# Projection and attention as one block, eight loads for each adapter pack, and the split of the base weights shared between VectorE and GpSimd

## The chip, the cores and the metric

One core of one Trainium2 chip. The metric is the device time of one launch in microseconds. The kernel before takes 848.53 us (median of three runs, 847.76 to 848.71).

## The reference

Input x has 8 sequences of 128 tokens with 512 features. Four stages follow one another, each adds its result to x:

```
x1 = x  + x  @ W0[id]^T                                  # one 512x512 base weight per sequence
x2 = x1 + attention(x1)                                  # 32 query heads, 8 key/value heads, D = 128, RoPE, causal
     q,k,v,o = x @ w + (x @ a[id]) @ b[id]               # rank-16 adapters a, b picked per sequence
x3 = x2 + (x2 @ B2[id]) @ A2[id]
out = x3 + x3 @ W3^T + b3 + 2 (x3 @ A3[id]) @ B3[id]
```

## The kernel before

Every float32 product is made of three products of rounded operands: each operand is split into a high part (a copy on ScalarE into the type float32r) and a low part (raw minus high, on VectorE or GpSimd), and TensorE adds hi*hi, hi*lo and lo*hi. The text calls these copies and low parts.

**First block (lines 210 to 768), 38 steps `s`.** At step s TensorE does the base product of sequence s (`product`, 12 matmuls), the adapter products `x1 @ a` of sequence s-1 (`adapters`), the transposition of x1 of sequence s (`turn_x1`, L693) and unit n = s-2 of the projections (`values`, `project`). Units 0 to 15 are values (two blocks of 512 columns, 8 sequences each, first matmul L730), units 16 to 31 keys, units 32 to 35 the queries of the first group (first matmul L78, `project`). The base weight of sequence s+1 is split at step s: ScalarE copies it in two halves (L391), VectorE makes the low parts (L491), and only then adds the product of sequence s to x (`add`, L497), for which `turn_x1` waits. For steps 1 to 7 the weight of the next sequence therefore stands in the chain of the step.

The raw base weights have three buffers (`w0_raw`), the adapters A three (`RAW = 3`). All loads of this block are issued by SyncE in one written order: `load_w0(b)` (xt and the base weight, 1 MB), `load_x`, `load_a`, and between them the projection blocks, `load_block_w` (1 MB, L166) and `load_block_b` (L176), which fills a **pack**. A pack holds the rows of the adapter B of all 8 sequences, each sequence's 16 rows four times (two for the high part and two for the low part), so that one more matmul per unit adds the adapter. `load_block_b` reads the id of each sequence and issues four loads of 16 partitions for it, 32 in all:

```
for quad in range(4):
    at = 32 * quad + R * (b % 2)
    dma.dma_start(raw_b[at:at + R, b // 2, :], src[bass.DynSlice(pick, 1), :, cols]...)
```

The first pack stands in SyncE's order ahead of `load_x(1)`, the second ahead of `load_w0(7)`, the third and fourth behind all base weights; the fourth stands ahead of the stores of rotated keys (`k_rot`, L348). The pack of the first queries comes from a tensor gathered by GpSimd (`bq_sel`) in four loads of 32 partitions (L180). `PIECES` says at which step each quarter of a block or pack is copied (ScalarE, L425 and L430) and gets its low part (VectorE, L514 and L519). Keys and first queries are rotated by VectorE (L609, L611) and added by GpSimd (L668). Values go to HBM by stores of ScalarE from three buffers.

**Second block (from line 770), 8 groups `g` of 8 slots.** A slot is one sequence of one group of four heads: scores (L1091), mask and maximum (VectorE), exponential (ScalarE), division (GpSimd, L966), transposition (L1100), values (L1108 to L1110), output projection with `wo` (L1122 to L1124) and its adapter `ao_pack` (L1131), and one query head of the next half (`queries`, `project`). Query heads are rotated by VectorE (L991, L993) and added by GpSimd (L959). Within the slots the weights of the next group are split: `wq` by ScalarE and GpSimd (L951), the query pack by ScalarE and VectorE (`bq_lo_part`, L999, low rows 64 to 127 only), `wo` by ScalarE, and its four low quarters by VectorE (0 in slot 1 and 1 in slot 2, L1004) and GpSimd (2 and 3 in slot 1, L976), followed by the low part of `ao_pack` (L979). `outputs` of slot 0 is issued in slot 2 and waits for the quarters one by one. Groups 1 to 6 are a hardware loop. Each block ends with a barrier of all engines. A third block makes the last two stages.

Of the kernel before, what the change touches and what calls it, by code (L numbers as in the profile page):

```python
# [7 lines left out]
P = 128  # L8
F32 = mybir.dt.float32
# [7 lines left out]
NEG = -1.0e30  # L17
# [13 lines left out]
def program(nc, x, xt, lora_ids, pos, attn_ids, slot_ids, mask, w0, wq, wk, wv, wo, a3, bq, bk, bv, ao, bo,  # L31
            l2a, l2b, w3, b3, l3a, l3b, ident_c, causal_c, rope_c, gather_c, twin_c, out):
# [20 lines left out]
    bq_sel = nc.dram_tensor("bq_sel", (B, R, KVH * GW), F32, kind="Internal").ap()  # L53
# [10 lines left out]
    with whole:  # L64
# [30 lines left out]
        twin = sb(whole, "twin", [P, 3])  # L95
        l2b_sel = sb(whole, "l2b_sel", [P, KC, B, R])
# [28 lines left out]
        axn = [sb(early, f"axn{i}", [P, 3, 4, 2, R], F32R) for i in range(2)]  # L125
# [9 lines left out]
        raw_b_in = sem(attn, "raw_b_in")  # L135
# [28 lines left out]

        def load_block_w(dma, j):
# [17 lines left out]
        RAW_B_IN = (512, 1024, 1536, 2048, 2048 + 64)  # L183

# [3 lines left out]
        def load_bq(dma, g, h):  # L188
            for quad in range(4):
                dma.dma_start(raw_b[32 * quad:32 * quad + 32, 2 * h:2 * h + 2, :],  # L190
                              bq_sel.rearrange("(c two) r n -> (two r) c n", two=2)[:, 2 * h:2 * h + 2, bass.DynSlice(g * GW, GW)]
                              ).then_inc(bq_in[h], 16)
# [12 lines left out]
        with ExitStack() as c:  # L205
            for i in (1, 2):
# [5 lines left out]
            RAW = 3  # L212
# [7 lines left out]
                     for flat, at in ((l2a_flat, 0), (l2a_flat, 3 * KC * R), (l2b_flat, 0))]  # L220
# [9 lines left out]
            ps_y = [ps(c, f"ps_y{i}", [P, HID]) for i in range(2)]  # L230
            ps_x1 = ps(c, "ps_x1", [P, KC, T])
            ps_ax = ps(c, "ps_ax", [P, 4, T])
            ps_a = ps_ax[:, 0, 0:3 * R].rearrange("p (n r) -> p n r", r=R)
            ps_at = ps_ax[:, 1:4, :]
            ps_p = [ps(c, f"ps_p{i}", [P, GW]) for i in range(4)]

            lora_ids_in = sem(c, "lora_ids_in")
            ids_in = sem(c, "ids_in")
            w0_first_in = [sem(c, f"w0_first_in{k}") for k in range(KC)]
            consts_in = sem(c, "consts_in")  # L240
            x_in = [sem(c, f"x_in{b}") for b in range(B)]
            xt_in = [sem(c, f"xt_in{i}") for i in range(RAW)]
            w0_in = [sem(c, f"w0_in{i}") for i in range(RAW)]
            a_in = [sem(c, f"a_in{b}") for b in range(B)]
            ident_ready = sem(c, "ident_ready")
            xt_hi_done = sem(c, "xt_hi_done")
            xt_lo_done = sem(c, "xt_lo_done")
            wt_hi_done = sem(c, "wt_hi_done")
            wt_lo_done = sem(c, "wt_lo_done")
            y_ready = sem(c, "y_ready")  # L250
            x1_done = sem(c, "x1_done")
            x1t_ready = sem(c, "x1t_ready")
            x1t_hi_done = sem(c, "x1t_hi_done")
            x1t_lo_done = sem(c, "x1t_lo_done")
            zeroed = sem(c, "zeroed")
            a_hi_done = sem(c, "a_hi_done")
# [1287 lines left out]
```

## Time and profile before

| | before |
|---|---|
| median of runs | 848.53 us |
| profiled execution, its own time | 849.5 us |
| its span | 847.8 us |
| TensorE matmul busy | 755.8 us (89%) |
| VectorE busy | 536.1 us (63%) |
| ScalarE busy | 324.8 us (38%) |
| GpSimd busy | 294.1 us (35%) |
| mean rate of transfers | 104 GB/s |
| mean granted TensorE clock | 0.956 of full speed |

The span is the time from the first to the last instruction; the execution's own time has 1.7 us more. Busy times overlap. A row of the timeline gives start, length, engine, line, operation, output and inputs, the count of merged instructions, and in brackets how long the engine sat idle before it and what ended that.

### The profile page before, as it was taken

The page shows a single profiled execution, that of the slowest core. Times are in us where ns is not written, and L with a number is a line of the kernel's source. Part 1 is how long each engine was busy: PE and PEld are TensorE (multiplying, and loading weights), DVE is VectorE, ACT ScalarE, POOL GpSimd, SP SyncE. Part 2 cuts the span into 40 slices and gives each one's busy share as a digit, 9 for nine tenths or more (in the row PEclk, how much of TensorE's full clock was granted, in tenths as well). Part 3 has the DMA queues.
Part 4 walks back from the last instruction along what each step waited for, and adds up shares of the span by engine and source line. Part 5 has one row for each costly group of instructions (what it writes and reads, how often), then busy time and mean ns, then how long its engine had stood idle before and what let it go on. Part 6 is the DMA issues. An engine that isn't in the chain of part 4 may idle for free. (4 is left out here: it accounts for less than half of the span.)

```text
span 847.8 us, 13367 instructions
## 1 busy us (share of the span) xinstructions
PE 755.8 (89%) x4100; PEld 623.1 (73%) x4100; DVE 536.1 (63%) x1370; ACT 324.8 (38%) x902; POOL 294.1 (35%) x265
## 2 busy tenths in 40 slices
PE   3292989879779999999999999999999999998798
PEld 2282877657567887887887888788788788876586
DVE  3251558756866667657566667666765756654883
ACT  4261525112053435335344435343534533433550
POOL 1020325253545236235326335423623532420220
PEclk8587899989889999999999999999999999999899
DMA  6573678546604122303303302312130310620502
GB/s 218 215 267 94 193 239 269 157 157 191 215 9 137 39 63 66 109 16 108 111 0 108 127 0 62 136 38 62 65 108 21 103 37 0 151 26 2 128 14 87
DMA packets 63083, 87.88 MB, mean 104 GB/s; under 512 B 20086, under 2 KB 37654, under 8 KB 59334
## 3 DMA queue, kind: packets, MB, share of 16 engines
q1 hardware_dynamic: 44338, 73.54, 28.0%
q10 hardware_dynamic: 17044, 8.46, 3.3%
q0 software_dynamic: 1664, 5.44, 2.1%
q8 instruction: 17, 0.28, 0.1%
q14 instruction: 20, 0.16, 0.1%
HBM read 72.45 MB, written 19.68 MB: 109 GB/s over the span
## 5 line engine op out<-in xcount | busy, mean ns | idle before, releaser
L966 POOL TENSOR_TENSOR prob<-prob,rinv 128x512 f32<-128x512 f32 x64 | 66.6, 1040 | 255.3 <-DVE rinv L1054 255.3
L907 ACT ACTIVATE ot_hi<-ps_o 128x512 fp32r<-128x512 f32 x64 | 38.1, 595 | 222.1 <-PE ps_o L1110 222.1
L1122 PE MATMUL ps_out<-wo_hi,ot_hi 128*128 128x512 f32 x256 | 102.8, 402 | 10.4 <-DVE wo_lo L1004 5.7
L959 POOL TENSOR_TENSOR qt<-qc,qs 128x512 f32<-128x512 f32 x60 | 77.9, 1298 | 70.0 <-DVE qs L993 70.0
L917 ACT ACTIVATE prob<-sm,nmax 128x128 f32<-128x128 f32 x256 | 99.8, 392 | 6.2 <-DVE nmax L1035 4.5
L1123 PE MATMUL ps_out<-wo_lo,ot_hi 128*128 128x512 f32 x256 | 101.3, 396 | 0.0
L1124 PE MATMUL ps_out<-wo_hi,ot_lo 128*128 128x512 f32 x256 | 100.8, 394 | 0.0
L78 PE MATMUL ps_q<-x1t_hi,wgt_hi 128*128 128x512 f32 x240 | 100.4, 418 | 0.0
L80 PE MATMUL ps_q<-x1t_hi,wgt_lo 128*128 128x512 f32 x240 | 95.4, 398 | 0.0
L79 PE MATMUL ps_q<-x1t_lo,wgt_hi 128*128 128x512 f32 x240 | 95.2, 397 | 0.0
L1032 DVE MEMSET gate<- 128x1 f32 x64 | 3.8, 59 | 136.9 <-PE ps_s L1091 136.9
L993 DVE TENSOR_TENSOR qs<-ps_q,trig 64x512 f32<-64x512 f32 x120 | 82.6, 689 | 3.7
L1091 PEld LDWEIGHTS ps_s<-kt,qt 128*128 128x128 f32 x512 | 66.6, 193 | 17.5 <-issue 10.3
L1091 PE MATMUL ps_s<-kt,qt 128*128 128x128 f32 x512 | 69.9, 280 | 7.5 <-PEq L286 6.8
L1122 PEld LDWEIGHTS ps_out<-wo_hi,ot_hi 128*128 128x128 f32 x256 | 48.2, 188 | 24.8 <-DVE wo_lo L1004 9.2
L1035 DVE CUSTOM_DVE_ANT_0 sm<-ps_s,maskbias 128x128 f32<-128x128 f32 x256 | 59.1, 286 | 0.9 <-issue 0.2
L1124 PEld LDWEIGHTS ps_out<-wo_hi,ot_lo 128*128 128x128 f32 x256 | 48.0, 187 | 11.6
L901 ACT ACTIVATE pt_hi<-ps_t 128x512 fp32r<-128x512 f32 x64 | 38.2, 596 | 44.1 <-PE ps_t L1100 44.1
L1123 PEld LDWEIGHTS ps_out<-wo_lo,ot_hi 128*128 128x128 f32 x256 | 48.3, 188 | 8.1
L80 PEld LDWEIGHTS ps_q<-x1t_hi,wgt_lo 128*128 128x128 f32 x240 | 45.4, 189 | 10.7
L78 PEld LDWEIGHTS ps_q<-x1t_hi,wgt_hi 128*128 128x128 f32 x240 | 45.8, 191 | 8.0
L79 PEld LDWEIGHTS ps_q<-x1t_lo,wgt_hi 128*128 128x128 f32 x240 | 45.7, 190 | 8.1
(193 smaller groups left out, 1720.2 us busy)
## 6 DMA issues: line engine op xcount, KB each, us to landing
raw_w<-in_wq SPq DMA_DIRECT2D x8, 1024.0 KB, 5.3
wo_raw<-in_wo SPq DMA_DIRECT2D x8, 1024.0 KB, 4.9
raw_b<-bq_sel SPq DMA_DIRECT2D x56, 128.0 KB, 5.2
qt<-in_w SPq DMA_DIRECT2D x5, 1024.0 KB, 6.8
v_hi_d<-v_hi ACTq DMA_DIRECT2D x16, 256.0 KB, 4.6
v_lo_d<-v_lo ACTq DMA_DIRECT2D x16, 256.0 KB, 5.1
kt<-k_rot SPq DMA_DIRECT2D x16, 256.0 KB, 2.6
v_hi<-v_hi_d SPq DMA_DIRECT2D x16, 256.0 KB, 3.2
```

What stands on the lines that cost most here:

```text
L78: pe.matmul(bank[:, :], w_hi[:, k, cols], x1t_hi[:, k, tok], start=(k == 0), stop=False)
L79: pe.matmul(bank[:, :], w_hi[:, k, cols], x1t_lo[:, k, tok], start=False, stop=False)
L80: pe.matmul(bank[:, :], w_lo[:, k, cols], x1t_hi[:, k, tok], start=False, stop=False)
L917: e = act.activation(prob[i][:, h, :], sm[:, h, :], ACT.Exp, bias=nmax[i][:, h:h + 1], scale=-1.0, accum_out=rsum[i][:, h:h + 1])
L959: pool.tensor_tensor(qt[:, half, h, :], qc[:, :], qs[:, :], ALU.add).then_inc(q_done, 1)
L966: pool.tensor_tensor(prob[i][:, :, :], prob[i][:, :, :], rinv[i][:, :].unsqueeze(2).broadcast_to([P, G, T]), ALU.mult).then_inc(prob_done, 1)
L993: dve.tensor_tensor(qs[to:to + 64, :], ps_q[i][at:at + 64, :], sin_t[to:to + 64, tok], ALU.mult).then_inc(q_mult, 1)
L1035: m = dve.tensor_tensor_reduce(out=sm[:, h, :], in0=ps_s[i][:, h, :], in1=maskbias[:, b, :], scale=-1.0, scalar=3.0e38, op0=ALU.add, op1=A ...
L1091: mm = pe.matmul(ps_s[b % 2][:, h, :], qt[:, half, h, at:at + T], kt[:, b * T:(b + 1) * T], start=True, stop=True)
L1122: pe.matmul(ps_out[:, :], ot_hi[:, q], wo_hi[:, h, :], start=(h == 0), stop=False)
L1123: pe.matmul(ps_out[:, :], ot_hi[:, q], wo_lo[:, h, :], start=False, stop=False)
L1124: pe.matmul(ps_out[:, :], ot_lo[:, q], wo_hi[:, h, :], start=False, stop=(h == G - 1))
```

## The change

It moves these things:

- The first and second block become one: the functions `project_sync`, `project_scalar` and so on are called at the head of each engine's part of the attention block, and the barrier between them is gone. The PSUM banks are shared between the parts (`ps_y` and `ps_s`, `ps_p` and `ps_out`, `ps_o`, `ps_q`), and explicit waits take the barrier's place.
- A pack has 8 loads of 64 partitions that read 16 rows four times, in each of the three places that fill `raw_b`. The order of rows in a pack changes with it, the low rows are no longer one half, and VectorE makes them with one instruction over 128 partitions. Each pair of sequences has a semaphore of its own.
- The first pack is spread: pair 0 behind `load_a(1)`, pair 1 behind `load_a(2)`, pairs 2 and 3 behind `load_a(3)`.
- GpSimd makes the last quarter of the low part of each base weight from the second on; VectorE makes three quarters.
- The adapters A have four raw buffers (`AR = 4`).
- In the attention loop `bq_lo_part` stands behind the rotation, VectorE makes one low quarter of `wo` a group and GpSimd three, and ScalarE copies all four quarters of `wo` ahead of `ot`.

```
-        def load_block_b(dma, j):
+        def load_block_b(dma, j, pairs):
...
-            for b in range(B):
+            for b in range(2 * pairs[0], 2 * pairs[-1] + 2):
                 pick = dma.value_load(id_rows[0:1, 1, b:b + 1], min_val=0, max_val=src.shape[0] - 1)
-                for quad in range(4):
-                    at = 32 * quad + R * (b % 2)
-                    dma.dma_start(raw_b[at:at + R, b // 2, :], src[bass.DynSlice(pick, 1), :, cols].rearrange("a r n -> (a r) n")).then_inc(raw_b_in, 16)
+                four_times(dma, b, src[bass.DynSlice(pick, 1), :, cols], raw_b_in[b // 2])
+
+        def four_times(dma, b, rows, done):
+
+            dma.dma_start(raw_b[4 * R * (b % 2):4 * R * (b % 2 + 1), b // 2, :], rows.broadcast_to([4, R, GW])).then_inc(done, 16)
...
         def load_bq(dma, g, h):
-            for quad in range(4):
-                dma.dma_start(raw_b[32 * quad:32 * quad + 32, 2 * h:2 * h + 2, :],
...
+            for b in range(HALF * h, HALF * (h + 1)):
+                four_times(dma, b, bq_sel[bass.DynSlice(g, 1), b], bq_in[h])
...
+                def split_w0_end(b):
+                    k = KC - 1
+                    pool.wait_ge(wt_hi_done, wt_parts(b, k))
+                    pool.tensor_tensor(wgt_lo[1 + b % 2][:, k, :], w0_raw[b % RAW][:, k, :], wgt_hi[1 + b % 2][:, k, :].bitcast(F32),
+                                       ALU.subtract).then_inc(wt_lo_end, 1)
...
+                        if b and k == KC - 1:
+                            pe.wait_ge(wt_lo_end, b)
...
                     def bq_lo_part(n, p):
                         dve.wait_ge(bq_hi_done, n)
-                        lo = slice(P // 2, P)
-                        dve.tensor_tensor(bq_pack[lo, p, :], bq_raw[lo, p, :], bq_pack[lo, p, :].bitcast(F32),
-                                           ALU.subtract).then_inc(bq_lo_done, 1)
+                        dve.scalar_tensor_tensor(bq_pack[:, p, :], bq_pack[:, p, :].bitcast(F32), lows[:, 0:1], bq_raw[:, p, :],
+                                                 ALU.mult, ALU.add).then_inc(bq_lo_done, 1)
...
                     def scores(t, g, b):
                         half = b // HALF
+                        if isinstance(t, int) and t == 0:
+                            pe.wait_ge(k_done, VU + G)
```

**SyncE, first loads.** Before, from the load of the first value block on (`raw_w<-in_wv`); the third base weight is the load `trig<-in_w`, and it comes after seven more groups like the one for `raw_b` shown here:

```order
L166 DMA raw_w<-in_wv 128x2048
L173 TENSOR_LOAD id_rows
L173 ISA x2
L176 ISA
L176 DMA raw_b<-in_bv 16x512 x4
L173 TENSOR_LOAD id_rows
L173 ISA x2
L176 ISA
L176 DMA raw_b<-in_bv 16x512 x4
```

Now, from the first load of the pack to the same base weight, behind `load_x(1)` and `load_a(1)`:

```order
L187 DMA raw_b<-in_bv 64x1x512
L182 TENSOR_LOAD id_rows
L182 ISA x2
L187 ISA
L187 DMA raw_b<-in_bv 64x1x512
L302 TENSOR_LOAD id_rows
L302 ISA x2
L313 DMA l3a_sel<-in_xt 128x512
L314 ISA
L314 DMA trig<-in_w 128x2048
```

Two loads of a pack stand ahead of the third base weight instead of 32, and `load_x(1)` stands ahead of both.

**VectorE, slot 1 of a group in the attention loop.** Before:

```order
L1008 TENSOR_TENSOR pt_lo<-ps_t,pt_hi 128x512
L999 TENSOR_TENSOR pack<-raw_b,pack 64x512
L1054 RECIPROCAL rinv<-rsum 128x4
L991 TENSOR_TENSOR qc<-ps_q,trig 128x512
L993 TENSOR_TENSOR qs<-ps_q,trig 64x512 x2
L1004 TENSOR_TENSOR wo_lo<-wo_raw,wo_hi 128x512
```

Now:

```order
L1022 TENSOR_TENSOR pt_lo<-ps_x_t,pt_hi 128x512
L1064 RECIPROCAL rinv<-rsum 128x4
L1006 TENSOR_TENSOR qc<-ps_p_q,trig 128x512
L1008 TENSOR_TENSOR qs<-ps_p_q,trig 64x512 x2
L1013 SCALAR_TENSOR_TENSOR pack<-pack,lows,raw_b 128x512
L1018 TENSOR_TENSOR wo_lo<-wo_raw,wo_hi 128x512
```

The low part of the pack has moved from ahead of the reciprocal to behind the rotation, and covers 128 partitions.

## Rows read from the trace of the kernel before

**Rows 1.** Waits of TensorE, 0 to 240 us: waited for, total, times, longest

```profile
PE ps_ax L716 <- DVE axn L507: 19.2, 3, 16.4
```

**Rows 2.** Timeline of TensorE: transpositions that open steps 1, 2, 3 and 7

```profile
41.41 1.12 PE L693 MATMUL ps_x<-ident,res 128*128 128x128 f32 x4 [16.16 <-DVE res L497]
...
51.76 0.66 PE L693 MATMUL ps_x<-ident,res 128*128 128x128 f32 x4
...
59.59 0.66 PE L693 MATMUL ps_x<-ident,res 128*128 128x128 f32 x4
...
110.12 0.66 PE L693 MATMUL ps_x<-ident,res 128*128 128x128 f32 x4
```

**Rows 3.** Timeline of SyncE's queue: issue start, length of all issues

```profile
10.37 19.34 SPq L176 DMA_DIRECT2D raw_b<-in_bv  x32
...
32.43 0.34 SPq L310 DMA_DIRECT2D trig<-in_w  x1
...
63.14 19.05 SPq L176 DMA_DIRECT2D raw_b<-in_bv  x32
...
155.88 19.70 SPq L176 DMA_DIRECT2D raw_b<-in_bk  x32
...
202.27 1.83 SPq L180 DMA_DIRECT2D raw_b<-bq_sel  x4
```

**Rows 4.** Timelines of ScalarE, VectorE and GpSimd: base weights, table loads

```profile
14.40 2.00 ACT L391 ACTIVATE wgt_hi<-qt 128x1024 fp32r<-128x1024 f32 x2 [1.90 <-DMA qt<-in_w]
...
37.31 1.06 ACT L391 ACTIVATE wgt_hi<-trig 128x1024 fp32r<-128x1024 f32 x1 [2.27 <-DMA trig<-in_w]
...
38.40 2.36 DVE L491 TENSOR_TENSOR wgt_lo<-trig,wgt_hi 128x1024 fp32r<-128x1024 f32 x2 [5.87 <-ACT wgt_hi L391]
...
62.36 1.06 ACT L391 ACTIVATE wgt_hi<-trig 128x1024 fp32r<-128x1024 f32 x1
...
99.67 0.55 POOL L650 DMA_DIRECT2D rope_cols<-in_rope_c  x1
...
110.88 0.75 DVE L527 TENSOR_SCALAR trig<-qt,rope_cols 128x1024 f32<-128x1024 int32 x1
```

**Rows 5.** One stretch: length, busy PE, PEld, DVE, ACT, POOL, clock, share, GB/s

```profile
60.00:65.00 5.00, 5.00 (x26) 4.18 (x25) 3.05 (x5) 4.26 (x8) 1.85 (x2) 1.00 1.02 342
```

**Rows 6.** Transfer issues by the page: count, size of each, us to landing

```profile
raw_b<-bq_sel SPq DMA_DIRECT2D x56, 128.0 KB, 5.2
...
raw_b<-bq_sel SPq DMA_DIRECT2D x4, 256.0 KB, 5.0
```

**Rows 7.** Timeline of TensorE: first matmul of key and query units

```profile
154.72 0.47 PE L78 MATMUL ps_p<-x1t_hi,wgt_hi 128*128 128x512 f32 x1 [3.37 <-DVE pack L519]
...
168.48 0.40 PE L78 MATMUL ps_p<-x1t_hi,wgt_hi 128*128 128x512 f32 x1
...
171.53 0.39 PE L78 MATMUL ps_p<-x1t_hi,wgt_hi 128*128 128x512 f32 x1
...
226.87 0.40 PE L78 MATMUL ps_p<-x1t_hi,wgt_hi 128*128 128x512 f32 x1
```

**Rows 8.** Timelines of TensorE and GpSimd at the block boundary

```profile
236.91 0.55 PE L1091 MATMUL ps_s<-kt,qt 128*128 128x128 f32 x1 [6.84 <-PEq L286]
...
232.32 1.26 POOL L668 TENSOR_TENSOR qt<-qt 128x512 f32<-128x512 f32 x1 [1.76 <-DVE qt L611]
```

**Rows 9.** Attention: TensorE's wait on `wo_lo` (whole run), and slots 1 and 2 of group 2

```profile
PE ps_out L1122 <- DVE wo_lo L1004: 5.7, 8, 0.9
...
383.18 0.69 DVE L999 TENSOR_TENSOR pack<-raw_b,pack 64x512 fp32r<-64x512 f32 x1
...
387.60 1.65 DVE L1004 TENSOR_TENSOR wo_lo<-wo_raw,wo_hi 128x512 fp32r<-128x512 f32 x1 [1.51 <-ACT wo_hi L891]
...
388.66 3.02 POOL L976 TENSOR_TENSOR wo_lo<-wo_raw,wo_hi 128x512 fp32r<-128x512 f32 x2
...
393.52 0.50 PE L1122 MATMUL ps_out<-wo_hi,ot_hi 128*128 128x512 f32 x1 [0.87 <-DVE wo_lo L1004]
```

More of the change, by code:

```diff
@@ L95, in program @@
         twin = sb(whole, "twin", [P, 3])
+        lows = sb(whole, "lows", [P, 1])
         l2b_sel = sb(whole, "l2b_sel", [P, KC, B, R])
@@ L124, in program @@
         a_lo = [sb(early, f"a_lo{i}", [P, KC, 3, R], F32R) for i in range(2)]
-        axn = [sb(early, f"axn{i}", [P, 3, 4, 2, R], F32R) for i in range(2)]
+        axn = [sb(early, f"axn{i}", [P, 3, 2, 4, R], F32R) for i in range(2)]
         early.close()
@@ L134, in program @@
         raw_w_in = sem(attn, "raw_w_in")
-        raw_b_in = sem(attn, "raw_b_in")
+        raw_b_in = [sem(attn, f"raw_b_in{p}") for p in range(PAIRS)]
         wq_in = sem(attn, "wq_in")
@@ L240, in program @@
[L240 to L249, printed above, removed]
@@ L274, in program @@
-            k_out = [sem(c, f"k_out{i}") for i in range(2)]
-            tables_in = sem(c, "tables_in")
-            tab = sem(c, "tab")
-            sines = sem(c, "sines")
+            ps_a = ps_ax[:, 0:3 * R].rearrange("p (n r) -> p n r", r=R)
+            ps_at = ps_ax[:, T:4 * T].rearrange("p (n t) -> p n t", t=T)
+            lora_ids_in = sem(attn, "lora_ids_in")
+            ids_in = sem(attn, "ids_in")
+            w0_first_in = [sem(attn, f"w0_first_in{k}") for k in range(KC)]
+            consts_in = sem(attn, "consts_in")
@@ new lines, in program @@
+            x_in = [sem(attn, f"x_in{b}") for b in range(B)]
+            xt_in = [sem(attn, f"xt_in{i}") for i in range(RAW)]
+            w0_in = [sem(attn, f"w0_in{i}") for i in range(RAW)]
+            a_in = [sem(attn, f"a_in{b}") for b in range(B)]
+            ident_ready = sem(attn, "ident_ready")
+            xt_hi_done = sem(attn, "xt_hi_done")
+            xt_lo_done = sem(attn, "xt_lo_done")
+            wt_hi_done = sem(attn, "wt_hi_done")
+            wt_lo_done = sem(attn, "wt_lo_done")
@@ L279, in parts @@
+            v_out = [sem(attn, f"v_out{i}") for i in range(VR)]
+            k_mult = sem(attn, "k_mult")
+            k_done = sem(attn, "k_done")
+            k_out = [sem(attn, f"k_out{i}") for i in range(2)]
+            tables_in = sem(attn, "tables_in")
+            tab = sem(attn, "tab")
+            sines = sem(attn, "sines")
             def parts(b):
@@ L920, in slots @@
                             if b < HALF and not last:
+                                if first and b == 0:
+                                    act.wait_ge(p_ready, KU + G)
                                 act.wait_ge(q_ready, B * g + b + 1)
@@ L931, in slots @@
                                     act.wait_ge(out_ready, B * g)
-                                wo_hi_part(g, 0)
-                                wo_hi_part(g, 2)
+                                for h in range(G):
+                                    wo_hi_part(g, h)
                             if not first or b >= 1:
@@ L1044, in slots @@
                                 pt(t - 1)
-                            if b == 2:
-                                wo_lo_part(g, 1)
-                            if not last and b % 2:
-                                bq_lo_part(PAIRS * g + b // 2 + 1, b // 2)
                             dve.wait_ge(exp_done, t + 1)
@@ L1056, in slots @@
                                 rotate(t, (b // HALF + 1) % 2, i)
+                            if not last and b % 2:
+                                bq_lo_part(PAIRS * g + b // 2 + 1, b // 2)
                             if b == 1:
```

989 lines of the change are left out of this document (491 added, 498 removed).

## The prediction

> **What bounds the kernel now.** Read the waits of TensorE over the first 240 us first. It is held 19.2 us by the adapter block `axn`, 16.4 of them at once [rows 1]; the row with 16.16 us in its brackets [rows 2] is a second hold, by `res`. TensorE is the busiest engine (89%), so idle time of it outside the attention loop is the time to be won. Those waits name VectorE, but VectorE is only the last link. The queue of SyncE shows the first one: the 32 loads of a pack take 19.34, 19.05 and 19.70 us to issue [rows 3], and whatever stands behind them in the program waits for that. The load of the third base weight goes out at 32.43 for this reason alone [rows 3], is copied from 37.31 on, and the transposition of step 1 starts 4.1 us later at 41.41 [rows 2, 4]. The pack issued from 63.14 does the same to the last base weight: TensorE's wait of 16.4 us on `axn` [rows 1]. The pack issued from 155.88 holds back the stores of rotated keys. In the attention loop TensorE works without pause except for one wait on `wo_lo` a group, 5.7 us in 8 places [rows 9].
>
> **Undisturbed pace, the yardstick for the sum.** In the first stage a step, from one transposition to the next, takes 51.76 to 59.59, 7.83 us, when nothing is late; right after the long hold it takes 41.41 to 51.76, 10.35 us, at TensorE's low level, so a hold costs 2.5 us more than itself [rows 2]. A key or query unit takes 3.05 us (168.48 to 171.53) [rows 7].
>
> **Issue of a pack.** A pack now has 8 loads. 32 loads in 19.34 us with 8 id reads; the four of one sequence therefore take 2.42 us. A load that carries 128 KB is issued in 1.83/4 = 0.46 us [rows 3], so the id read is about 2.42 - 4 x 0.41 = 0.8 us and a pack costs 8 x (0.8 + 0.4) = 9.6 us instead of 19.3. Only one pair of the first pack stands ahead of the third base weight, which then goes out near 14.7 instead of 32.43.
>
> **How long a pack occupies the transfer engines.** The trace has no load of 64 partitions that reads 16 rows four times, so bound it. At the rate of a full queue, 342 GB/s in 60 to 65 us [rows 5], its 1.05 MB take 3.1 us. Two batches of four 128 KB loads, each landing 5.2 us after its issue [rows 6], give about 10.4 us at most. Nearest is the pack of four 256 KB loads at 202.27: the same tile, whole, with 32 partitions each; issued over 1.8 us and landing 5.0 after [rows 3, 6], near 7 us. I take 7.4 and keep 3.1 and 10.4 as ends. The Trainium skill, "DMA: Bandwidth & Descriptors", Rules for kernel authors, speaks against this form of load: an outermost dimension of c copies confines a transfer to at most c of the 16 engines, here 4. By it, an estimate from that page and the 342 GB/s, a pack takes 12 us and the sum comes out some 9 us later than mine; no row shows such a transfer.
>
> **Step 1.** The second base weight landed at 14.40 [rows 4]. Behind it now stand x and the adapter A of sequence 0, the first value block, x and A of sequence 1, xt and the third base weight: 3.08 MB by their shapes, 9.0 us at 342 GB/s, and a quarter of a pack, 1.85 us. It lands at 25.2. From landing to the transposition the trace has 4.1 us; VectorE's second low part is half as long (1.2 to 0.6 us [rows 4], the last quarter goes to GpSimd beside it), so 3.5 us: 28.7 instead of 41.41. **Gain 12.7.** In undisturbed steps that same 0.6 us is worth nothing: TensorE is busy throughout, and it covers VectorE.
>
> **Steps 2 to 7.** Each step needs its weight about 3 us after the transposition that opens it (59.59, copy at 62.36 [rows 2, 4]; I allow 0.2 us more). A sequence's transfers are 1.67 MB, 4.9 us; a value block 3.1 us; a step's two stores 1.5 us. Landings: third 25.2, fourth 25.2 + 4.9 + 1.85 = 32.0, fifth (half a pack and a store) 42.1, sixth 48.5, seventh (value block) 58.0, eighth (a whole pack) 71.8. Transpositions at 28.7, 39.0 (10.35 later, for TensorE has just been held), 46.9, 54.7 and 62.5, so the weights are needed at 31.7, 42.0, 49.9, 57.7 and 65.5. All but the eighth come within 0.3 us. The eighth is 6.3 us late; with 2.5 us of low clock the transposition of step 7 starts at 39.0 + 5 x 7.83 + 6.3 + 2.5 = 87.0 instead of 110.12 [rows 2]. That is 23.1 less, so **10.4 more**. GpSimd now splits a last quarter before it issues the table loads, some 3.5 us later by my estimate (it waits for ScalarE's second copy of the step, then works 1.3 us). It issued the last at 99.67 and VectorE first used them at 110.88 [rows 4]; 11.2 less 3.5 still covers a landing of 5 to 6 us, so I cost it at nothing, and a longer landing would show in full.
>
> **Values to the first key unit.** Gathers, value stores, tables and the waits around 148 to 154 us stand in the same order with the same bytes. I take 0.
>
> **Keys and first queries.** From 154.72 to 226.87 are 18 units in 72.15 us [rows 7]; undisturbed 18 x 3.05 = 54.9. Loss 17.3, of which 1.5 us is the low clock after the wait that ends at 154.72 and stays. The rest came from the pack at 155.88 and from the query pack at 202.27. The first now frees SyncE near 165.5 instead of 175.6. GpSimd wants the first key store's landing about then, and TensorE runs four banks ahead. The query pack now has a semaphore for each pair, so two pairs are enough to start. I give back 0.8 us for stores that queue behind a pack: **15.0**. VectorE's low part over all 128 partitions is priced as over 64: the time goes by the 512 columns.
>
> **The boundary.** TensorE restarts at 236.91 after 6.84 us [rows 8]. Without a block boundary the scores still need the last rotated query, which GpSimd makes at 232.32 + 1.26 = 233.6 [rows 8]; the last unit ended near 230.1 (236.91 - 6.84): **3.3**. Late next is that rotation itself.
>
> **Attention.** VectorE no longer makes the second quarter of `wo_lo` late in slot 2; GpSimd makes three in slot 1. It did two from 388.66 in 3.02 us [rows 9]; a third and the adapter part at 1.3 each end at 394.3. TensorE had been ready for the second quarter at 392.65 and reaches the adapter 2.1 us later, 394.7: just covered. So the waits of 0.87 in six groups and their restart, 1.1 a group with the weight load, go: 6.6. Against that, `bq_lo` moves behind the rotation, where it meets GpSimd's addition. One such meeting is in the trace, 1.65 us for a VectorE part that takes 0.69 alone [rows 9]. The Trainium skill, "SBUF — State Buffer", Who interferes with whom, has it that the one that starts second is fully blocked when both read two tiles of SBUF; by that GpSimd would be 0.7 us later at each meeting. In the trace GpSimd's surplus at such a meeting is 0.5 us at most (two quarters in 3.02 us, 1.3 each alone). It can reach TensorE at the two slots of a group whose scores need the rotation just made, and part of it is made up by a reciprocal 0.7 us earlier: of 0 to 0.5 I take 0.2 x 13 = 2.6. **Net 4.0.**
>
> **Sum.** 23.1 + 15.0 + 3.3 + 4.0 = 45.4 us. 847.8 - 45.4 = 802.4 span; the profiled execution took 849.5, 1.7 more than its span and 1.0 more than the median of 848.53, so 803.1: **803**.
>
> **Rivals.**
> *Packs at full rate.* If four copies spread as any load, a pack takes 3.1 us and the eighth weight lands 8.6 us earlier: no hold in steps 2 to 7, and no low clock; step 1 gains 1.1 more. Then 803 - 6.3 - 2.5 - 1.1 - 1 (keys) = 792. For it: 2 KB rows throughout, as before. Against: the pack at 202.27 took twice that.
> *Packs at 10.4 us or more.* Two packs lie before the eighth weight: 2 x 3 = 6 us, and about 2 in keys: 811. It decides if a 128 KB load holds its engines over 1.3 us.
> *Issue does not shrink.* If the issue time went by rows, 64 against 16, a pack would still take 19 us. Left are the new place of the first pair (about 10), the boundary and attention: 803 + 24 = 827. Against it: loads of 128 partitions are issued in the same 0.3 to 0.5 us.
> *Slower: the lock in the attention loop.* 28 slots get the moved part behind the rotation. If each meeting cost both its surpluses, 1.65 - 0.69 = 0.96 on VectorE and 3.02 - 2 x 1.28 = 0.46 on GpSimd [rows 9], and all of it reached TensorE, and GpSimd's third quarter cost 1.3 in each of 8 groups on top, the loop would lose 28 x 1.42 + 10.4 = 50 us instead of gaining 4.0; the kernel would take 848.5 - 41.4 + 50 = 857. It decides from 41 us on, 0.7 us a slot. Against: at most 2 of 8 slots wait for a rotation at all.
>
> **Chances.** The forecast 0.50, full rate 0.25, slow packs 0.17, issue unchanged 0.05, lock 0.03. A measurement of this kernel tells about 0.2%, 1.7 us, from no change; the first four are all faster by more: faster 0.97, same 0, slower 0.03. The range runs from 5 us under the full-rate case to 5 us over the slow packs, 787 to 816, and leaves out the last two cases and tails of the others.
>
> **What would show it.** The pack's issue near 9.6 us; the third base weight issued near 15 and the transposition of step 1 near 29; a single hold before step 6 of about 6 us and none elsewhere in the first stage; no wait over 1 us among the keys after the first two; scores 3.5 us after the last query unit; no wait on `wo_lo`. A hold of 12 us means slow packs, none at all means full rate. Wrong would be a longer stretch between the last base product and the first key, which I left untouched, or slots over 8.4 us.

## The result, and the profile after

| | before | change |
|---|---|---|
| median of runs (lowest to highest) | 848.62 us (847.76 to 851.34) | 822.80 us (820.86 to 829.19) |
| ratio to before, 95% interval | | 0.9704, 0.9646 to 0.9761 |
| profiled execution, its span | 847.8 us | 819.2 us |
| TensorE matmul busy | 755.8 us (89%) | 752.1 us (92%) |

The kernel became faster, by 26 us where 45 were forecast; 822.8 lies above the range of 787 to 816. The two spans differ by 28.6 us. Cut at the same five places in both traces they show where the gain is and where it is missing (the last column is the first experiment below):

| stretch | before | forecast | change | rows outermost |
|---|---|---|---|---|
| start to the transposition of step 1 | 41.41 | 28.7 | 29.38 | 29.14 |
| on to the transposition of step 7 | 68.71 | 58.3 | 59.36 | 52.50 |
| on to the second key unit | 44.60 | 44.6 | 46.82 | 43.22 |
| on to the last query unit (18 units) | 72.15 | 57.2 | 74.34 | 63.88 |
| on to the first scores | 10.04 | 6.7 | 6.76 | 6.76 |
| on to the end of the span | 610.9 | 606.9 | 602.5 | 606.9 |

So the first stage and the boundary came nearly as forecast, the loop gave more, and the keys, from which I expected 15.0 us, lost 2.2. The table is of one profiled execution each; the change's repeat (experiment 5) has 30.43, 61.03, 44.51 and 72.54 us in the first four stretches. The rows behind that begin with SyncE's queue in the change (start, length of the issues, engine and line, output and input, count), to be held against [rows 3]:

```profile
12.20 2.69 SPq L187 DMA_DIRECT2D raw_b<-in_bv  x2
16.52 0.35 SPq L314 DMA_DIRECT2D trig<-in_w  x1
...
51.44 14.41 SPq L187 DMA_DIRECT2D raw_b<-in_bv  x8
67.56 0.35 SPq L314 DMA_DIRECT2D qt<-in_w  x1
...
136.68 13.75 SPq L187 DMA_DIRECT2D raw_b<-in_bk  x8
...
179.44 4.62 SPq L187 DMA_DIRECT2D raw_b<-bq_sel  x8
```

The third base weight (`trig`) goes out at 16.52 instead of 32.43, as meant. But a pack of eight loads takes about 14 us to issue, not 9.6. The transpositions that open steps 1 and 7, in TensorE's timeline, against 41.41 and 110.12 in [rows 2]:

```profile
29.38 1.12 PE L708 MATMUL ps_x_t<-ident,res 128*128 128x128 f32 x4 [2.83 <-DVE res L502]
...
88.74 0.66 PE L708 MATMUL ps_x_t<-ident,res 128*128 128x128 f32 x4
```

TensorE's waits from 0 to 240 us, grouped (waited for, total, times, longest), against [rows 1]: the 16.4 us are gone, and the longest outside the start is now 9.3 us, among the queries.

```profile
PE ps_p_o L78 <- DVE pack L524: 15.5, 3, 9.3
PE ps_x_t L708 <- DVE res L502: 10.7, 3, 6.5
...
PE ps_ax_ao L731 <- DVE axn L512: 7.0, 3, 4.2
PE ps_y_s L1109 <- POOL qt L682: 3.6, 1, 3.6
```

Follow the 9.3 us back, first to the pack. VectorE makes its low part from a copy by ScalarE, whose timeline reads:

```profile
184.79 0.63 ACT L437 ACTIVATE pack<-raw_b 128x512 fp32r<-128x512 f32 x1 [13.64 <-DMA raw_b<-bq_sel]
187.52 0.63 ACT L437 ACTIVATE pack<-raw_b 128x512 fp32r<-128x512 f32 x1 [2.10 <-DMA raw_b<-bq_sel]
190.19 0.63 ACT L437 ACTIVATE pack<-raw_b 128x512 fp32r<-128x512 f32 x1 [2.04 <-DMA raw_b<-bq_sel]
192.87 0.63 ACT L437 ACTIVATE pack<-raw_b 128x512 fp32r<-128x512 f32 x1 [2.04 <-DMA raw_b<-bq_sel]
```

Each copy waits for its own pair's loads and not for SyncE, which had issued all eight by 184.06. The copies start 2.7 us apart: 1.35 us for a load of 128 KB, 10.8 us for a pack. The view by stretches (bounds, length, busy PE, PEld, DVE, ACT, POOL, clock, DMA share, GB/s) shows how, in two stretches in which hardly anything but a pack is in flight:

```profile
57.00:60.00 3.00, 3.00 (x23) 2.78 (x22) 0.80 (x2) 0.00 (x0) 1.25 (x1) 1.00 0.27 101
...
190.00:193.00 3.00, 2.59 (x13) 1.94 (x11) 0.00 (x0) 0.77 (x2) 0.00 (x0) 1.00 0.26 96
```

The mean busy share of the 16 transfer engines is a quarter: four are at work. The rule of the Trainium skill, "DMA: Bandwidth & Descriptors", Rules for kernel authors, that c copies outermost leave a transfer at most c engines, agrees with this trace: 0.27 and 0.26. Whatever is queued behind such a pack is late too. GpSimd, which may reuse a buffer only when its store of rotated keys has landed, waited 9.95 and 8.82 us for one, behind the packs issued at 136.68 and 179.44 (in the kernel before, 13.49 us behind the pack issued at 155.88):

```profile
156.32 1.28 POOL L682 TENSOR_TENSOR l2a_sel<-qt 128x512 f32<-128x512 f32 x1 [9.95 <-DMA k_rot<-l2a_sel]
...
193.52 1.26 POOL L682 TENSOR_TENSOR l2b_sel<-qt 128x512 f32<-128x512 f32 x1 [8.82 <-DMA k_rot<-l2b_sel]
```

In the first wait the issue has its part: SyncE sent that store at 150.48, 13.8 us after the pack's first load, and it landed 5.8 us later. The second store left at 184.11 and took 9.3 us to land, where a key store takes 2.4 to 2.9 by the median. VectorE's timeline shows that this store, and not the pack's own pairs, sets the end of TensorE's wait:

```profile
194.88 0.69 DVE L616 TENSOR_TENSOR qt<-ps_p_o,trig 128x512 f32<-128x512 f32 x1 [5.70 <-POOL l2b_sel L682]
...
199.87 1.86 DVE L524 SCALAR_TENSOR_TENSOR pack<-pack,lows,raw_b 128x512 fp32r<-128x512 f32 x1
```

ScalarE had copied the last pair by 193.50. VectorE made its low part only from 199.87 on, because it stood 5.70 us for GpSimd and then had two rotations and the third pair ahead of it.

TensorE's second query unit starts after 9.28 us of idle time, and that unit takes 4.99 us instead of 3.04, for the granted clock is 0.50 from 201.87 to 204.00 (1.00 again from 207.00):

```profile
201.87 0.77 PE L78 MATMUL ps_p_o<-x1t_hi,wgt_hi 128*128 128x512 f32 x1 [9.28 <-DVE pack L524]
206.86 0.40 PE L78 MATMUL ps_p_q<-x1t_hi,wgt_hi 128*128 128x512 f32 x1
209.90 0.40 PE L78 MATMUL ps_p_q<-x1t_hi,wgt_hi 128*128 128x512 f32 x1
```

### The profile page after: what moved, and what is told of

The parts are those of the page before. It is cut to its first block and busy times, and to the rows that moved or that the text cites. A ratio compares the mean times of both kernels' runs of the same rounds, so it can differ in the third digit from the quotient of the medians.

```text
span 819.2 us, 13219 instructions
## 1 busy us (share of the span) xinstructions
PE 752.1 (92%) x4100; PEld 625.0 (76%) x4100; DVE 543.8 (66%) x1362; ACT 324.1 (40%) x902; POOL 325.6 (40%) x280
## 5 line engine op out<-in xcount | busy, mean ns | idle before, releaser
L78 PE MATMUL ps_p_q<-x1t_hi,wgt_hi 128*128 128x512 f32 x280 | 115.9, 414 | 0.8 <-DVE qt L618 0.8
L80 PE MATMUL ps_p_q<-x1t_hi,wgt_lo 128*128 128x512 f32 x280 | 110.9, 396 | 0.0
L79 PE MATMUL ps_p_q<-x1t_lo,wgt_hi 128*128 128x512 f32 x280 | 110.8, 396 | 0.0
L1140 PE MATMUL ps_p_out<-wo_hi,ot_hi 128*128 128x512 f32 x256 | 101.9, 398 | 6.6 <-DVE ot_lo L1026 4.7
L1141 PE MATMUL ps_p_out<-wo_lo,ot_hi 128*128 128x512 f32 x256 | 101.4, 396 | 0.0
L1142 PE MATMUL ps_p_out<-wo_hi,ot_lo 128*128 128x512 f32 x256 | 100.8, 394 | 0.0
L1008 DVE TENSOR_TENSOR qs<-ps_p_q,trig 64x512 f32<-64x512 f32 x120 | 82.6, 688 | 3.7
L1049 DVE CUSTOM_DVE_ANT_0 sm<-ps_y_s,maskbias 128x128 f32<-128x128 f32 x256 | 59.0, 286 | 31.4 <-issue 31.0
L1109 PEld LDWEIGHTS ps_y_s<-kt,qt 128*128 128x128 f32 x512 | 67.1, 193 | 12.4 <-POOL qt L682 3.8
L1109 PE MATMUL ps_y_s<-kt,qt 128*128 128x128 f32 x512 | 69.0, 278 | 4.9 <-POOL qt L682 3.6
L78 PEld LDWEIGHTS ps_p_q<-x1t_hi,wgt_hi 128*128 128x128 f32 x280 | 53.3, 190 | 10.3 <-DVE qt L618 1.0
```

What stands on the lines that cost most here:

```text
L78: pe.matmul(bank[:, :], w_hi[:, k, cols], x1t_hi[:, k, tok], start=(k == 0), stop=False)
L79: pe.matmul(bank[:, :], w_hi[:, k, cols], x1t_lo[:, k, tok], start=False, stop=False)
L80: pe.matmul(bank[:, :], w_lo[:, k, cols], x1t_hi[:, k, tok], start=False, stop=False)
L1008: dve.tensor_tensor(qs[to:to + 64, :], ps_q[i][at:at + 64, :], sin_t[to:to + 64, tok], ALU.mult).then_inc(q_mult, 1)
L1049: m = dve.tensor_tensor_reduce(out=sm[:, h, :], in0=ps_s[i][:, h, :], in1=maskbias[:, b, :], scale=-1.0, scalar=3.0e38, op0=ALU.add, op1=A ...
L1109: mm = pe.matmul(ps_s[b % 2][:, h, :], qt[:, half, h, at:at + T], kt[:, b * T:(b + 1) * T], start=True, stop=True)
```

## The experiments

A ratio is to the kernel before, timed beside the variant; where two variants are compared, it is through their ratios.

**1. Rows outermost.** In a pack, partition 4r+q now holds copy q of row r (it was 16q+r), so the same eight loads have 16 rows outermost. `axn` and the constant `lows` follow.

```
-axn = [... [P, 3, 2, 4, R] ...]
+axn = [... [P, 3, 2, R, 4] ...]
-raw_b[...] <- rows.broadcast_to([4, R, GW])
+raw_b[...] <- rows.rearrange("a r n -> r a n").broadcast_to([R, 4, GW])
-lows = np.where(p % (4 * R_PACK) >= 2 * R_PACK, -1.0, 0.0)
+lows = np.where(p % 4 >= 2, -1.0, 0.0)
```

> Edit: the four copies of each adapter row stand next to each other in a pack (partition 4r+q instead of 16q+r), so that the source of the same 8 loads has 16 rows outermost instead of 4 copies; bytes, load count and issue order are those of the change. Theory A (a load with four copies outermost keeps to 4 of the 16 transfer engines, so a pack lands one 128 KB load every 1.34 us, 10.7 us in all, and what is queued behind it is late): ScalarE's copies of the query pack, now 2.7 us apart at 184.79, 187.52, 190.19 and 192.87, come as fast as ScalarE works (under 1.2 us apart); TensorE's wait of 9.28 us before the unit at 201.87 falls under 3 us, that of 4.18 us at 60.68 under 1.5 us; the stretch from the key unit at 135.56 to the query unit at 209.90 falls from 74.3 to 64 to 67 us; time 822.8 less 12 to 16, near 808. Rival B (SyncE's 14 us of issue a pack is what delays the rest, the landing rate is not): issue stays at 13.7 to 14.4 us, both waits stay within 1 us of what they are, time 820 to 824.

Measured: 801.01 us, ratio 0.9415 (0.9394 to 0.9435), against 0.9704 for the change. The copies of the query pack come 1.2 us apart, and the transfer engines are three quarters busy. ScalarE's timeline:

```profile
165.98 0.63 ACT L437 ACTIVATE pack<-raw_b 128x512 fp32r<-128x512 f32 x1 [12.16 <-DMA raw_b<-bq_sel]
167.24 0.63 ACT L437 ACTIVATE pack<-raw_b 128x512 fp32r<-128x512 f32 x1 [0.62 <-DMA raw_b<-bq_sel]
168.42 0.63 ACT L437 ACTIVATE pack<-raw_b 128x512 fp32r<-128x512 f32 x1 [0.55 <-DMA raw_b<-bq_sel]
```

Two stretches in which the pack lands, in the same view as above:

```profile
166.00:168.00 2.00, 2.00 (x11) 1.68 (x10) 1.94 (x4) 1.25 (x2) 1.66 (x1) 1.00 0.71 244
168.00:170.00 2.00, 2.00 (x10) 1.60 (x10) 1.94 (x4) 1.06 (x2) 0.00 (x0) 1.00 0.79 293
```

The hold of 4.18 us behind the transposition of step 4 is gone from TensorE's timeline (a wait of 1.99 us ends at 72.20), and the 18 key and query units take 63.88 us instead of 74.34. The time fell by 21.8 us where theory A gave 12 to 16. For the query pack theory A holds against rival B: its issue did not shrink, its copies came faster and the wait behind it fell. One thing neither had foreseen: the issue of a pack with id reads fell too, from 14.1 to some 10.3 us, in SyncE's timeline:

```profile
47.76 10.55 SPq L187 DMA_DIRECT2D raw_b<-in_bv  x8
...
162.40 5.04 SPq L187 DMA_DIRECT2D raw_b<-bq_sel  x8
```

So for the three packs with id reads, faster issue and faster landing come together, and no run separates them. In the change such a pack issues a load every 1.9 us or so, against the 1.35 us that a load takes to move; of the two, the issue is the slower there. Behind the second key pack the key store now goes out 10.3 us after the pack's first load and GpSimd has it 2.7 us later, against 13.8 and 5.8: about half of what that store gained is issue, half is landing.

One wait of theory A did not fall as far as it said: the second query unit still stood for 3.50 us, and it took 5.51 us itself, at a granted clock of 0.50 until 183.00.

```profile
180.20 0.77 PE L78 MATMUL ps_p_o<-x1t_hi,wgt_hi 128*128 128x512 f32 x1 [3.50 <-DVE pack L524]
185.71 0.40 PE L78 MATMUL ps_p_q<-x1t_hi,wgt_hi 128*128 128x512 f32 x1
```

**2. Only the query pack spread.** Copies outermost everywhere, but the pack issued at 179.44 goes in eight loads of 16 rows for all four pairs.

```
-for b in range(B): four_times(sp, b, bq_sel[0:1, b], ...)
+for at in range(0, P, R):
+    sp.dma_start(raw_b[at:at + R, :, :], bq_sel[0].rearrange("(c two) r n -> two r c n", two=2)[at // (4 * R)])
```

> Edit: only the query pack of the first stretch (issued at 179.44) is loaded otherwise: still 8 loads of 128 KB, but each carries one of the 8 groups of 16 rows for all four pairs, so its outermost dimension is 16 rows; the first copy waits for all eight. Theory A (confined landing, with the key stores behind it): GpSimd's wait of 8.82 us for the store of rotated keys and TensorE's 9.28 us fall by 6 to 9 us, with 2 us of low clock after it; nothing changes before 179 us; time 822.8 less 8 to 11, near 813. Theory A without the stores (the pack's own pairs are late, stores do not matter): about the same for TensorE, but GpSimd's wait stays over 6 us. Rival C (TensorE's 9.28 us is set by VectorE and GpSimd being busy, not by any landing): the wait stays over 7 us, time 820 to 824.

Measured: 820.21 us, ratio 0.968 (0.9622 to 0.9738), which is not told apart from the change. TensorE's 9.28 us became 5.39 before the first query unit and 0.91 before the second, and GpSimd's 8.82 became 5.12. TensorE's timeline:

```profile
190.87 0.77 PE L78 MATMUL ps_p_out<-x1t_hi,wgt_hi 128*128 128x512 f32 x1 [5.39 <-DVE pack L526]
```

GpSimd's timeline:

```profile
186.09 1.27 POOL L684 TENSOR_TENSOR l2b_sel<-qt 128x512 f32<-128x512 f32 x1 [5.12 <-DMA k_rot<-l2b_sel]
```

By the ratios the gain is 2 us, where I gave it 8 to 11. Part of the reason is in the edit: the first query unit now waits for all eight loads. Another part shows in the view by stretches while the pack lands:

```profile
178.00:180.00 2.00, 1.22 (x7) 0.88 (x6) 1.94 (x4) 0.00 (x0) 0.83 (x1) 1.00 1.09 134
...
182.00:184.00 2.00, 2.00 (x11) 1.64 (x10) 0.00 (x0) 0.00 (x0) 0.00 (x0) 1.00 1.10 136
```

All the engines are busy, yet they move 134 to 136 GB/s, half of what experiment 1's loads do. These loads write 16 partitions each, those 64; that this is the reason was not tested. At that rate a pack takes 7.8 us. And the key pack before it is as slow as ever; behind it GpSimd still waits 8.82 us for a store, at 152.56. So theory A's mechanism is seen here, but its price is not: only the packs taken together gave 24 us (experiment 1).

**3. VectorE makes the whole low part.** `split_w0_end` on GpSimd and its waits are taken out.

> Edit: VectorE makes all four quarters of each base weight's low part again, GpSimd none; the rest is the change. Theory D (the share given to GpSimd shortens the path from landing to product only where a weight is late, steps 1, 2 and 3, by 0.6 us each, and is free elsewhere): transposition of step 1 at 30.7 instead of 30.15, that of step 3 at 51.5 to 52.5 instead of 50.17, time 822.8 plus 1 to 2.5, near 824.5. Rival E (the two engines stand in each other's way, VectorE's part taking 1.56 us and GpSimd's 1.8 us where they meet, so the split gives nothing): within 1 us of 822.8 or faster.

Measured: 826.59 us, ratio 0.9733 (0.9702 to 0.9764), 2.5 us above the change by the ratios, inside both intervals. The transposition of step 1 starts at 29.49; in the change's two profiles (the first and that of experiment 5) it does so at 29.38 and 30.43. The quarter's 0.6 us is smaller than that scatter, so neither theory D nor rival E is shown. It was tried again in the better form (experiment 9).

**4. The queries' low part ahead of the reciprocal again.** `bq_lo_part` returns to its old place in VectorE's slot.

> Edit: the low part of the adapter B for queries stands ahead of the reciprocal again, as before the change; the rest is the change. My prediction put the move behind the rotation at a loss of 2.6 us (0 to 6.5) in the attention loop. If so, undoing it gives 2.6 us back, near 820. Rival F (the loop gained 8.4 us instead of the 4.0 forecast because the move is itself a gain: reciprocal, probabilities and transposition come 0.7 us earlier in four slots of a group): undoing it costs 3 to 6 us, 826 to 829. If neither, within 1 us of 822.8.

Measured: 819.06 us, ratio 0.9631 (0.9599 to 0.9663); the intervals overlap at their edges. A group of the loop takes 67.25 us. Rival F, by which undoing the move costs 3 to 6 us, falls; what the move itself costs is read from the loops below (experiments 5 and 6).

**5. The change again.** No edit.

> Edit: none, the change itself once more beside the kernels of this call. Two executions of the same attention loop differ: groups of 67.5 us in the change's profile, 68.06 us in the two with the loads spread over rows, whose loop is the same. If that is only how two executions differ, this one lies anywhere from 67.4 to 68.1 and the time from 821 to 826. If the loop is slower for the other row order of a pack, this one repeats 67.5 within 0.1.

Measured: 823.87 us, ratio 0.9696 (0.9666 to 0.9727). Groups of 68.08 us, so the 67.5 us of the first profile were one execution's luck, and so are about 4 to 6 of the 8.4 us that it has over the kernel before. The page's group of GpSimd's rotation (busy, mean ns; idle before) shows what differs. Here, in the repeat:

```profile
L973 POOL TENSOR_TENSOR qt<-qc,qs 128x512 f32<-128x512 f32 x60 | 92.7, 1546 | 79.1 <-DVE qs L1008 79.1
```

In the change's first profile:

```profile
L973 POOL TENSOR_TENSOR qt<-qc,qs 128x512 f32<-128x512 f32 x60 | 83.7, 1395 | 77.8 <-DVE qs L1008 77.8
```

The single instructions tell what the averages hide. Of the 60 additions 28 meet VectorE's low part of the pack, which starts 0.05 us ahead of them, and in each meeting exactly one of the two is long. Both kinds stand in the timelines of the change's first profile, VectorE's:

```profile
296.26 0.75 DVE L1013 SCALAR_TENSOR_TENSOR pack<-pack,lows,raw_b 128x512 fp32r<-128x512 f32 x1
...
313.03 1.89 DVE L1013 SCALAR_TENSOR_TENSOR pack<-pack,lows,raw_b 128x512 fp32r<-128x512 f32 x1
```

and GpSimd's:

```profile
296.31 1.85 POOL L973 TENSOR_TENSOR qt<-qc,qs 128x512 f32<-128x512 f32 x1 [1.46 <-DVE qs L1008]
...
313.07 1.29 POOL L973 TENSOR_TENSOR qt<-qc,qs 128x512 f32<-128x512 f32 x1 [1.46 <-DVE qs L1008]
```

GpSimd is the long one in 11 of the 28 in that profile, in 27 in the repeat and in 26 in experiment 1; the loops take 521.8, 528.2 and 525.8 us. The loop is shortest where it is mostly VectorE that is held up.

**6. Rows outermost and the low part early.** Experiments 1 and 4 together.

> Edit: rows outermost in the pack loads, and the low part of the queries' adapter B ahead of the reciprocal again. Theory (the first gain is in the first stage and the keys, the second 0.3 to 0.8 us in each of eight groups of the loop, so they add): 801.0 less 3 to 6, near 797; groups of the loop at 67.3 us instead of 68.06, the first 250 us as with rows outermost alone. Rival (the gain of 3.7 us of the second edit was scatter): 799 to 802, groups at 67.9 to 68.1.

Measured: 796.02 us, ratio 0.9372 (0.934 to 0.9404). Groups of 67.28 us, and in the page's group GpSimd's rotation at 1298 ns:

```profile
L973 POOL TENSOR_TENSOR qt<-qc,qs 128x512 f32<-128x512 f32 x60 | 77.9, 1298 | 63.3 <-DVE qs L1008 63.3
```

In this loop no addition meets a low part. TensorE's waits (217 to 710 us) show a part of the gain. In the repeat of the change, which this one is held against:

```profile
PE ps_y_s L1109 <- POOL qt L973: 2.3, 9, 0.3
PE ps_p_out L1140 <- DVE ot_lo L1026: 2.3, 1, 2.3
```

The first of these waits does not occur in this experiment; it is 2.3 us of the 7.6 by which the two loops differ, and the rest is not traced to a wait. From the first scores to the last slot's, its loop takes 520.6 us, and that of experiment 1, which differs by this edit alone, 525.8.

**7. Query packs in four loads of 256 KB, and 8. the first of them issued two stores earlier.**

```
-four_times(dma, b, ...)   # 8 loads, 16 rows outermost
+dma.dma_start(raw_b[:, p, :], pair_rows.unsqueeze(1).broadcast_to([2 * R, 4, GW]))   # 4 loads, 32 rows outermost
...
-if m == 8:
+if m == 6:
```

> Edit: as the one before, and the query packs are loaded with 4 loads of 256 KB (the 32 rows of a pair outermost, four copies of each) instead of 8 of 128 KB. Theory G (SyncE's 5.0 us for eight loads is on the path of the first query pack, whose pairs landed 1.2 us apart): the issue of the pack at 162.40 falls from 5.0 to about 2, its last pair lands 1 to 2 us earlier, TensorE's wait of 3.50 us before the second query unit falls by 0 to 1.5 us, since VectorE's queue (rotation, then one low part a step) stands in it too: near 796. Rival (VectorE alone sets it): no change against the one before, within 1 us.

> Edit: as the one before, and the first query pack is issued behind the seventh store of keys instead of the ninth. Theory H (what is left of the loss among the keys, 9.0 us over 18 undisturbed units, comes to 6.5 us from the query pack that is issued at 162.40, since SyncE stands at the store of the ninth key unit till then, and lands beside VectorE's rotations): issued near 151.2, landed by 157, no wait of TensorE over 1 us from the second key unit to the scores except where a key store's landing is late; 5 to 6.5 us off, near 790. Rival (the low parts on VectorE stand behind its rotations in any case, 0.75 us alone and 1.88 us where they meet GpSimd): at most 2 us off, near 794.

Measured: 796.61 us, ratio 0.9386 (0.935 to 0.9422), and 794.80 us, ratio 0.9365 (0.9332 to 0.9397). The issue fell to 2.55 us and the early pack went out at 152.48, long before it was wanted, and neither moved the time beyond its interval. TensorE's wait at the second query unit was 1.38 us in experiment 6, 2.34 in the seventh and 1.22 in the eighth. So the 9.0 us of loss that I read from experiment 1's one profile were not steady: experiment 6's 18 units take 58.22 us. Theories G and H fall; what is left there is VectorE's queue or chance.

**9. VectorE whole, in the best form, beside that form once more.**

> Edit: rows outermost, the queries' low part ahead of the reciprocal, and VectorE makes all four quarters of each base weight's low part, GpSimd none. In the change itself that last edit gave 826.6 against 822.8 and 823.9 on other chips, with intervals that overlap. Theory D (a quarter on GpSimd is worth 0.6 us wherever a weight is late, which with rows outermost is step 1 alone): 796 plus 0.5 to 1.5. Rival E (the two engines block each other, so it gives nothing or costs): 794 to 796. Rival (GpSimd's share is worth more, since VectorE's queue is the limit of every step of the first stage): 799 or more, with waits on res in steps 3 to 7.

> Edit: rows outermost and the queries' low part ahead of the reciprocal, once more and with more rounds, beside the one before: 794 to 798, ratio to the kernel before 0.937 to 0.940.

Measured: 796.59 us, ratio 0.9374 (0.935 to 0.9398), with VectorE alone, and 794.80 us, ratio 0.9357 (0.9334 to 0.938), with the quarter on GpSimd. The quarter on GpSimd gives 1.4 us here and 2.5 in experiment 3, both within the intervals; its sign isn't shown. Rows outermost with the low part early is the best form found, and experiments 7 and 8 are level with it: 54 us under the kernel before, 28 under the change.

**10. What sets the number of engines.** Rows are outermost elsewhere and only the query pack's source is changed, bytes and packets being equal. The first kernel leaves out half of the adapter rows of the first group's queries, the second three quarters:

```
 e8: bq_sel[0:1, b, 0:8].broadcast_to([8, 8, GW])             # 8 copies outermost, 8 rows inner
 e9: bq_sel[0, b, 0:4].unsqueeze(1).broadcast_to([4, 16, GW])  # 4 rows outermost, 16 copies inner
```

> Edit: rows outermost in the pack loads as before, except the query pack of the first stretch: each of its 8 loads (128 KB, 64 packets of 2 KB as ever) has 8 copies outermost of 8 rows. It leaves out half of the adapter rows of the first group's queries. Theory (a load is spread over as many of the 16 transfer engines as its outermost dimension counts, each load on the same ones): the stretch in which only this pack is in flight shows a DMA share near 0.5 and near 200 GB/s, and ScalarE's copies of the pairs come 1.3 to 1.4 us apart, against 0.26, 98 GB/s and 2.70 us with four copies. Rival (what slows the load is that the same rows are read again and again): share near 0.25 again, copies 2.5 us or more apart. Rival (load size or queue, not its shape): as with rows outermost, share 0.7 to 0.8.

> Edit: as the one before, but each load of that query pack has 4 rows outermost, each copied 16 times in the inner dimension. It leaves out three quarters of the adapter rows of the first group's queries. Theory (the count of the outermost dimension alone decides): share 0.25 to 0.28, 96 to 101 GB/s, ScalarE's copies of the pairs 2.7 us apart, although no copy is outermost; issue of the pack 4.6 to 5.6 us; TensorE's wait at the second query unit back at 7 to 9 us. Rival (copies outermost are what slows it, a row that is read 16 times in a row is not): share 0.7 to 0.8, copies 1.2 us apart, the wait under 4 us.

With 8 outermost the stretch with the pack alone reads, in the view by stretches:

```profile
164.00:166.00 2.00, 2.00 (x12) 1.63 (x11) 1.97 (x3) 0.00 (x0) 0.76 (x1) 1.00 0.49 147
166.00:168.00 2.00, 2.00 (x11) 1.57 (x10) 1.94 (x4) 0.00 (x0) 0.56 (x1) 1.00 0.52 156
```

With 4 rows outermost, ScalarE's timeline:

```profile
166.22 0.63 ACT L437 ACTIVATE pack<-raw_b 128x512 fp32r<-128x512 f32 x1 [14.04 <-DMA raw_b<-bq_sel]
168.91 0.63 ACT L437 ACTIVATE pack<-raw_b 128x512 fp32r<-128x512 f32 x1 [2.06 <-DMA raw_b<-bq_sel]
171.56 0.63 ACT L437 ACTIVATE pack<-raw_b 128x512 fp32r<-128x512 f32 x1 [2.02 <-DMA raw_b<-bq_sel]
```

And a stretch of it:

```profile
170.00:172.00 2.00, 2.00 (x12) 1.64 (x11) 0.59 (x1) 0.44 (x1) 0.00 (x0) 1.00 0.27 96
```

Half the engines with 8, a quarter with 4 rows, and with these TensorE's wait is back at 8.12 us, although the pack's issue is 4.83 us: here landing alone brings it back. Copies as such are not slow: 16 or 32 rows outermost, each read four times, go at three quarters of the engines and more. The count of the outermost dimension decides, and later loads do not turn to the idle engines. With 8 engines the rate was 150 GB/s, not the 200 expected, so the pairs came 1.9 us apart and not 1.35. The two kernels took 805.29 and 804.51 us, one timing each, beside 850.54 for the kernel before. By the ratios that is 4.5 and 3.7 us over experiment 1, so the shape of the query pack alone is worth some 4 us; the other 20 or so of experiment 1's 24 us would then lie mostly with the packs that read ids, where issue and landing are not told apart.

## Why the prediction was wrong, by its own steps

- **Step 1, 12.7 us:** 12.0 measured (11.0 in the repeat). Right.
- **Steps 2 to 7, 10.4 us more:** 9.4 measured (7.7 in the repeat). The size was nearly right and the path wrong. I had TensorE's 16.4 us [rows 1] hang on the last base weight, and ScalarE's timeline of the kernel before says otherwise:

```profile
83.61 0.63 ACT L430 ACTIVATE pack<-raw_b 128x512 fp32r<-128x512 f32 x1 [18.42 <-DMA raw_b<-in_bv]
...
97.22 1.05 ACT L391 ACTIVATE wgt_hi<-qt 128x1024 fp32r<-128x1024 f32 x1
```

ScalarE stood 18.42 us for the pack itself, and the copy for which `axn` waits stands behind the pack's in its queue; the last base weight was copied at 97.22 without a wait. In the change the hold at 60.68 is one of 4.18 us, and again ScalarE stood at the second pack's own pairs (waits of 4.15 and 2.04 us on `raw_b`); the eighth base weight was copied at 75.83 without a wait. So the hold of 12 us that was to show slow packs never came, though the packs were slow. With packs on all engines steps 2 to 7 take 52.50 us, 5.8 less than forecast; my full-rate rival had 8.8 less.
- **Issue of a pack, 9.6 us:** 14.1 us with copies outermost, 10.3 with rows outermost. The estimate was near for a load that spreads, and 4.5 us short for the change's; it came from loads of 16 partitions that the kernel before issues.
- **The occupation of the transfer engines, 7.4 us a pack:** this is the term that failed, together with the 0.8 us for what stands behind a pack (below). It is 10.8 us, just over the end that I had called "about 10.4 us at most". I took the pack at 202.27 as nearest because tile and bytes were the same; its loads have 32 partitions outermost, and the shape counted, not the bytes. The sentence on the Trainium skill's rule, 12 us a pack, had it nearly right, and the rule deserved the forecast, for the change's source has four copies outermost in plain sight.
- **Values to the first key unit, 0:** from the value unit of step 7 to the first key unit it is 37.72 us (89.15 to 126.87), and 37.54 before (110.54 to 148.08). Right; from the first to the second key unit 2.1 us were lost, 0.5 to a longer wait, the rest to low clock (0.57 granted from 127 to 131).
- **Keys and first queries, 15.0 us:** minus 2.2. I gave back 0.8 us for stores behind a pack, and my slow-pack rival 2 us. They were worth more: with rows outermost the same stretch is 10.5 us shorter in its profile. A pack that occupies a quarter of the engines for 10.8 us delays what is queued behind it on them. Behind the query pack that is the key store that GpSimd waits for, and through GpSimd and VectorE TensorE's 9.28 us, with a slow unit after them: 11.2 us at one place. Behind the second key pack the longer issue comes to it. That is why the rival came to 811 and the kernel to 823, although its condition, over 1.3 us a load, was met (1.35).
- **The boundary, 3.3 us:** 3.28 measured; the late thing is the rotation, 3.56 us before the scores. Right.
- **Attention, 4.0 us net:** 8.4 in the first profile; from the first scores to the last slot's the loop takes 530.2 us before, 521.8 in that profile, 528.2 in the repeat and 525.8 in experiment 1. The net is 2 to 5 us, with one execution at 8. Its parts were both too small: with `bq_lo` in its old place the loop takes 521.5 and 520.6 us (experiments 4 and 6), 9 less than before and not 6.6, and `bq_lo` behind the rotation costs 4 to 7 (experiments 1 to 3 and 5; nothing in the change's first profile), near the upper end of 6.5 that I kept, not 2.6. GpSimd's addition takes 1546 ns with it and 1298 without, and the 28 that meet it bear all of that: a meeting makes GpSimd's 1.29 us into 1.86, 0.57 more, or VectorE's 0.75 into 1.89, 1.14 more, and in none of the 28 both. The Trainium skill, "SBUF — State Buffer", Who interferes with whom, by which the one that starts second is fully blocked, would make it 0.7 at each meeting. The trace agrees that one of the two is held up and the other not, but not on who: VectorE starts first by 0.05 us in all 28 and is the one held up in 17 of the first profile.

The sum of the forecast, 45.4 us, is what experiment 1's profile shows (45.4). That is partly chance: its first stage gave 5 us more than my terms and its keys 7 less.

**What stays open.** Why the id reads cost 1.2 us each beside a load on four engines (14.1 less 4.6 us, in eight) and 0.65 beside one that spreads (10.3 less 5.0). How the 20 us or so that are left for the packs with id reads divide between their issue and their landing. What decides in a meeting whether GpSimd or VectorE is held up, and with it whether the groups take 67.5 or 68.06 us. Why loads of 16 rows into 16 partitions move 135 GB/s on all engines.

## What to carry to other kernels

Fewer and larger loads help fully only if each spreads over the transfer engines. Look at the outermost dimension of the access pattern first: put the longest one there, and lay out the partitions so that copies are inner. Read the rate too: experiment 2's loads kept all engines busy and moved half as much. To test for it in a trace, take a stretch with that load alone and read the DMA share; a value near c/16 gives it away. When a queue is made shorter by its issue time, price the landings behind it as well: stores that hand back a buffer sit in the same line. And when a wait is put down to a load, look at what its engine was doing when the load had landed.

## What was not expected of the hardware

- Four engines moved 96 to 101 GB/s, some 24 GB/s each; eight moved 147 to 156, some 19 each. Loads of 128 KB into 16 partitions moved 134 to 136 with all of them busy (experiment 2).
- SyncE's issue of eight loads with id reads took 13.75 to 14.41 us when they went to four engines, and 10.0 to 10.6 us when they spread; eight loads without id reads took 4.6 and 5.0.
- Where VectorE's low part (two inputs in SBUF, 0.75 us alone) and GpSimd's addition of 128x512 (1.29 us alone) start 0.05 us apart, one of them is long and never both: 1.86 us on GpSimd or 1.89 on VectorE. Which one it is differs between executions of one kernel, 11 to 17 in one and 27 to 1 in the other.
